# A kernel for graph diffusion, routed experts and segment paths: path columns packed two to a word and kept in registers

## The chip, the cores and the metric

One core of a Trainium2 chip runs the whole program. The metric is the device time of one execution in microseconds; of several executions the median counts.
## What is computed

The reference has four steps with a residual each. Cut to what matters here:

```python
x = x + gnn_diffusion(layernorm(x), ...)          # step 1
x = x + routed_experts(layernorm(x), ...)         # step 2
# step 3: 64 paths over 16 segments of 32 columns, for 4352 edges
x1 = x_nodes[src].reshape(-1, 16, 32)             # x_nodes = layernorm(x), 256 x 512
x2 = x_edges.reshape(-1, 16, 32)
i1, i2, i3 = path_indices[:, 0], path_indices[:, 1], path_indices[:, 2]
contrib = path_coeffs[None, :, None] * x1[:, i1, :] * x2[:, i2, :]
edge_out = zeros.at[:, i3, :].add(contrib)
out = zeros.at[dst].add(edge_out.reshape(-1, 512))
x = x + out
x = x + grouped_experts(layernorm(x), ...)        # step 4
```

The path indices are data: the kernel learns only at run time which segments a path reads and writes.

## The kernel before

The 4352 edges lie as 34 tiles of 128 edges, and step 3 works them in three blocks of 10, 14 and 10 tiles (`BLOCKS`, L35). For each block all 64 paths (`NP`) are worked in turn, so there are 192 path steps.

- VectorE multiplies (L744): the gathered node columns of segment i1, the edge columns of segment i2 and the path's coefficient go into one of seven slots of `prod` (`SLOTS`). Then it adds the slot's later tiles into the sums in on-chip memory (L758). It works multiply(p + 1) before add(p). A multiply waits until TensorE has used the slot seven paths back (`psums`); an add waits for the add before it (`sums`).
- TensorE adds the slot's first four tiles (L1042), in blocks 0 and 1 a fifth too (L1045), into banks of PSUM by an identity matmul at column i3, once the multiply is done (`mults`). Between paths it gathers node rows for the next block (L972, six matmuls a tile) and scatters the last block's sums to nodes (L993, four matmul records a tile), at path numbers fixed by `gather_paths` and `scatter_paths`: gathers after paths 3, 7, 11, 15, 20 and so on up to 58 in block 0; in block 1 a scatter after paths 1, 7, 13 and so on and a gather after paths 3, 9, 15 and so on, ten of each; in block 2 a scatter after paths 1, 5, 9 and so on.
- ScalarE copies gathered rows out of PSUM (L443), makes the one-hot matrices of the scatter (L448, L451), and between blocks copies the PSUM sums (L479, L483). TensorE closes a block with matmuls of zeros (L1055), waits for these copies and opens the next with matmuls of zeros (L1037).

The columns of a path come from registers. VectorE packs the three segment numbers of a path into one integer of three 9-bit fields, times 32 (L565 to L569). Each of the two engines loads 16 such words at a time into registers (`load_words`, L183): the first 16 ahead of the blocks, then VectorE at p % 16 == 4 (L765) and TensorE at p % 16 == 7 (L1053), twelve loads on each in all. `column` (L187) takes a field out with // and %, which become register operations of the sequencer, as does the address arithmetic around them. [...]

Ahead of step 2 TensorE works its last matmuls of step 1 (L928), then 34 small matmuls that only keep it busy (`keep_warm`, L850, called by `transpose_xn`, L855), and waits for the normalised rows that VectorE makes (L533) to transpose them (L858).

## Time and profile before

| | us |
|---|---|
| median of 3 executions (328.79 to 329.98) | 329.12 |
| the profiled execution's own time | 329.91 |
| its span, first to last instruction | 328.1 |
| PE matmul busy | 304.3 (93%) |
| DVE busy | 237.4 (72%) |
| ACT busy | 87.5 (27%) |
| path steps, block 0 | about 106 to 156 |
| path steps, block 1 | about 156 to 220.5 |
| path steps, block 2 | about 220.5 to 272 |

Busy shares are averages over stages with different limits, so they are read by stretch. Matmul ends are modelled: a matmul's duration overlaps the next one, and what one costs is read from start to start. The same holds for VectorE, whose instructions overlap at their ends.

### The profile page before, as it was taken

The numbers are of one execution on the slowest core, as the hardware profiler recorded it, in microseconds if no ns is written. First come the engines' busy times: TensorE is split into PE (matmuls) and PEld (weight loads), VectorE is DVE, ScalarE is ACT, GpSimd is POOL, SyncE is SP. The second block draws the span as 40 slices with busy tenths as digits, with TensorE's granted clock in tenths as the row PEclk, the third lists the DMA queues.
The fourth block names the chain that finished last, engine by engine and source line by source line (L and its number), as shares of the span: only waits on it lengthen the run. The fifth ranks groups of instructions, "written<-read, shape, count | busy, mean of one in ns | idle before, by whom it ended". The sixth has DMA issues, their size and how long they took to land.

```text
span 328.1 us, 5513 instructions
## 1 busy us (share of the span) xinstructions
PE 304.3 (93%) x1813; PEld 205.6 (63%) x1828; DVE 237.4 (72%) x637; ACT 87.5 (27%) x173; POOL 17.8 (5%) x24
## 2 busy tenths in 40 slices
PE   3898999999998998999799999988988998999996
PEld 2665598876443686877476766664655554477832
DVE  1998944121354999989999999997999995766131
ACT  3600241002115111211422222128322237512120
POOL 3000050000003000000000000030000004000000
PEclk9999999999999999999999999996999999999999
DMA  5999900000052000000000000019700007200001
GB/s 128 406 396 444 391 12 0 2 1 1 0 222 99 0 3 0 2 1 2 1 2 0 1 2 0 3 29 392 301 0 0 3 0 248 75 0 2 2 0 64
DMA packets 8845, 26.55 MB, mean 81 GB/s; under 512 B 2673, under 2 KB 2674, under 8 KB 7922
## 3 DMA queue, kind: packets, MB, share of 16 engines
q1 hardware_dynamic: 7328, 26.12, 20.6%
q8 instruction: 15, 0.25, 0.3%
q10 hardware_dynamic: 1490, 0.09, 0.3%
q14 instruction: 12, 0.10, 0.1%
HBM read 25.68 MB, written 0.52 MB: 80 GB/s over the span
## 4 chain that ended last, share of the span: by engine, by line
PE 78%; DVE 8%; ACT 4%; issue 3%; DVEq 2%; another core or an unknown queue 2%; DMA 1%; SPq 0%; ACTq 0%
PE psum L1042 14%; PE psum L993 12%; PE psum L972 12%; PE psum L946 9%; PE psum L1045 5%; PE psum L967 4%; PE psum L850 4%; DVE prod L744 3%; PE psum L882 2%; PE psum L1101 2%; PE psum L1126 2%; PE psum L1120 2%; PE psum L898 2%; ACT big L479 2%; DVE big L758 2%
## 5 line engine op out<-in xcount | busy, mean ns | idle before, releaser
L744 DVE SCALAR_TENSOR_TENSOR prod<-big,coef_b,edges 128x320 f32 (+1 forms) x192 | 113.2, 591 | 2.4 <-PE psum L1042 1.0
L1042 PE MATMUL psum<-prod,ident 128*128 128x128 f32 x384 | 77.0, 301 | 6.4 <-DVE prod L744 5.6
L758 DVE TENSOR_TENSOR big<-big,prod 128x160 f32 (+2 forms) x192 | 71.9, 374 | 7.7 <-issue 6.9
L1042 PEld LDWEIGHTS psum<-prod,ident 128*128 128x128 f32 x384 | 59.8, 192 | 26.6 <-issue 22.6
L993 PE MATMUL psum<-big,dst_oh 128*128 128x512 f32 x116 | 55.8, 607 | 0.4 <-ACT dst_oh L451 0.4
L972 PE MATMUL psum<-xparts,src_t 128*128 128x512 bf16 x192 | 45.9, 379 | 0.6
L1045 PE MATMUL psum<-prod,ident 128*128 128x32 f32 x256 | 39.3, 236 | 0.0
L1045 PEld LDWEIGHTS psum<-prod,ident 128*128 128x128 f32 x256 | 38.9, 192 | 0.0
L972 PEld LDWEIGHTS psum<-xparts,src_t 128*128 128x128 bf16 x204 | 20.3, 108 | 18.7 <-issue 0.6
L443 ACT ACTIVATE big<-psum 128x512 f32<-128x512 f32 x29 | 17.0, 598 | 56.2 <-PE psum L972 56.2
L993 PEld LDWEIGHTS psum<-big,dst_oh 128*128 128x128 f32 x116 | 20.4, 194 | 17.3 <-issue 14.7
L448 ACT ACTIVATE dst_oh<-iota_b,idx_f 128x256 f32<-128x256 bf16 x29 | 14.7, 505 | 60.2 <-PE psum L993 60.2
L946 PE MATMUL psum<-edges,big 128*128 128x256 f32 x128 | 28.6, 381 | 0.0
L946 PEld LDWEIGHTS psum<-edges,big 128*128 128x128 f32 x128 | 24.0, 190 | 3.8 <-DVE edges L696 0.3
L850 PE MATMUL psum<-iota_b,zero_b 128*128 128x256 bf16 x137 | 18.0, 284 | 0.0
L356 POOL MEMSET big<- 128x2560 f32 (+2 forms) x3 | 8.8, 2939 | 164.2 <-PE psum L993 112.7
L850 PEld LDWEIGHTS psum<-iota_b,zero_b 128*128 128x128 bf16 x137 | 13.8, 102 | 3.0 <-issue 0.7
L967 PE MATMUL psum<-big,edges 128*128 128x512 f32 x32 | 14.0, 596 | 0.0
L451 ACT ACTIVATE dst_oh<-dst_oh 128x256 f32<-128x256 f32 x29 | 12.1, 417 | 0.9
L967 PEld LDWEIGHTS psum<-big,edges 128*128 128x128 f32 x32 | 6.0, 190 | 7.5 <-issue 7.5
L696 DVE TENSOR_TENSOR edges<-edges,psum 128x256 f32<-128x256 f32 x8 | 3.2, 415 | 10.3 <-ACT edges L427 10.3
L427 ACT ACTIVATE edges<-psum 128x256 f32<-128x256 f32 x8 | 3.1, 383 | 26.3 <-PE psum L946 22.2
(167 smaller groups left out, 264.3 us busy)
## 6 DMA issues: line engine op xcount, KB each, us to landing
big<-in_w SPq DMA_DIRECT2D x3, 2048.0 KB, 19.2
edges<-in_edge SPq DMA_DIRECT2D x2, 2560.0 KB, 18.0
edges<-in_f SPq DMA_DIRECT2D x1, 4096.0 KB, 12.9
edges<-in_edge SPq DMA_DIRECT2D x1, 3584.0 KB, 23.2
edges<-in_f SPq DMA_DIRECT2D x1, 2560.0 KB, 9.9
edges<-in_f SPq DMA_DIRECT2D x1, 1536.0 KB, 17.2
big<-in_gnn_w SPq DMA_DIRECT2D x1, 1024.0 KB, 10.3
xs<-in_x SPq DMA_DIRECT2D x1, 512.0 KB, 5.2
```

Of the source, the lines that this page charges most:

```text
L443: nc.scalar.activation(x1g[b % 2][:, t - FIRST[b], :], gather_bank(t), ACT.Copy).then_inc(gathered, 1)
L448: nc.scalar.activation(to, iota_b[:], ACT.Abs, bias=idx_f[:, 0, t:t + 1]).then_inc(dist_made, 1)
L451: nc.scalar.activation(to, to, ACT.Relu, scale=-1.0, bias=1.0).then_inc(done, 1)
L744: nc.vector.scalar_tensor_tensor(out=prod[:, (p0 + p) % SLOTS, 0:tiles], in0=xg[:, 0:tiles, bass.ds(i1, U)], scalar=coef_b[:, p:p + 1], in ...
L758: nc.vector.tensor_tensor(v, v, prod[:, (p0 + p) % SLOTS, KEPT[b]:tiles], ALU.add).then_inc(sums, 1)
L850: mm(to[:, 0:N], zero_b[:], iota_b[:], start=True, stop=True)
L946: last = mm(bank[2 + c % 4][:, n * N:(n + 1) * N], w[:, kc, c * P:(c + 1) * P], xnT[:, kc, :], start=kc == 0, stop=kc == KC - 1)
L967: last = mm(bank[2 + h], hT[:, c, h * P:(h + 1) * P], w2_sb[:, c, :], start=c == 0, stop=c == HC - 1)
L972: last = mm(gather_bank(t), src_t[:, h, t * P:(t + 1) * P], xparts[:, k, h, :], start=h == 0 and k == 0, stop=h == H - 1 and k == 2)
L993: last = mm(bank[2 + h], dst_oh[:, n % DR, h * P:(h + 1) * P], tile_sums(b, t), start=n == 0, stop=False)
L1042: last = mm(path_sums(to), ident[:], prod[:, slot, 0:PT].rearrange("p t u -> p (t u)"), start=False, stop=False, skip_group_check=True)
L1045: last = mm(psum[:, bass.ds(to + 512, U)], ident[:], prod[:, slot, PT, :], start=False, stop=False, skip_group_check=True)
```

## The change

Two paths share a word: the packing uses fields of 4 bits (`SEG`), 12 bits a path, two paths side by side and all times 32, and needs one packing instruction more. There are 32 words (`path_pair`). Each engine loads all of them once, VectorE ahead of the first copies of gathered rows, TensorE ahead of `transpose_xn(1)`, where 24 small matmuls take the place of 34; all later loads are gone. `column` extracts with shifts and masks, in another form in each block (shift, then mask; mask, then shift; shift, mask, shift back), so that no extracted value is one that the program already has.

```diff
@@ -36,8 +36,10 @@
     FIRST = [0, 10, 24]
     KEPT = [5, 5, 4]
     PT = 4
-    SB = (NS * U).bit_length() - 1
-    PG = 16
+    SEG = (NS - 1).bit_length()
+    FIELD = (NS - 1) * U
+    PAIRS = NP // 2
+    assert U == 32
     NB = len(BLOCKS)
     QT = -(-T // 4)
     BMAX = max(BLOCKS)
@@ -77,6 +79,7 @@
         zero_b = sb("zero_b", [P, P], BF16)
         coef_b = sb("coef_b", [P, NP])
         path_w = sb("path_w", [1, NP], I32)
+        path_pair = sb("path_pair", [1, PAIRS], I32)
         idx_f = sb("idx_f", [P, 2, T])
         stats = sb("stats", [P, H, 6])
         mv = sb("mv", [P, H, 2])
@@ -177,21 +180,22 @@
         hid_bd = take([FC, NG * EQ])
         made_rows = take([QF, H, D])
 
-        def load_words(engine, words, n):
-
-            regs = [engine.alloc_register(f"{engine.engine.name}_word{i}") for i in range(n, n + PG)]
-            engine.load(regs, path_w[0:1, n % NP:n % NP + PG])
-            for i, r in enumerate(regs):
-                words[n + i] = engine.snap(r, donate=True, min_val=0, max_val=2 ** (3 * SB) - 1)
-
-        def column(words, n, k):
-
-            v = words[n]
-            if k:
-                v = v // 2 ** (SB * k)
-            if k < 2:
-                v = v % 2 ** SB
-            return nc.s_assert_within(v, 0, (NS - 1) * U,
+        def load_words(engine):
+            regs = [engine.alloc_register(f"{engine.engine.name}_word{i}") for i in range(PAIRS)]
+            engine.load(regs, path_pair[0:1, :])
+            return [engine.snap(r, donate=True, min_val=0, max_val=U * 2 ** (6 * SEG) - 1) for r in regs]
+
+        def column(words, b, p, k):
+
+            shift = SEG * (3 * (p % 2) + k)
+            v = words[p // 2]
+            if b == 0:
+                v = (v >> shift) & FIELD if shift else v & FIELD
+            elif b == 1:
+                v = (v & (FIELD << shift)) >> shift if shift else v & (FIELD + (1 << 29))
+            else:
+                v = ((v >> (shift + 5)) & (NS - 1)) << 5
+            return nc.s_assert_within(v, 0, FIELD,
                                       skip_runtime_bounds_check_because="segment numbers are below the segments")
 
         def scatter_order(b):
@@ -562,11 +566,15 @@
             nc.vector.tensor_scalar(idx_f[:, 0, :], idx_f[:, 1, :], -1.0, None, ALU.mult).then_inc(neg_ready, 1)
             dve.wait_ge(path_in, 16)
             pw = path_w[:].rearrange("o (n k) -> o n k", k=1)
-            link(nc.vector.scalar_tensor_tensor(out=pw, in0=path_i[:, :, 2:3], scalar=float(NS * U), in1=path_i[:, :, 1:2],
+            link(nc.vector.scalar_tensor_tensor(out=pw, in0=path_i[:, :, 2:3], scalar=float(NS), in1=path_i[:, :, 1:2],
                                                 op0=ALU.mult, op1=ALU.add))
-            link(nc.vector.scalar_tensor_tensor(out=pw, in0=pw, scalar=float(NS * U), in1=path_i[:, :, 0:1],
+            link(nc.vector.scalar_tensor_tensor(out=pw, in0=pw, scalar=float(NS), in1=path_i[:, :, 0:1],
                                                 op0=ALU.mult, op1=ALU.add))
-            nc.vector.tensor_scalar(pw, pw, float(U), None, ALU.mult).then_inc(packed, 1)
+            pp = path_pair[:].rearrange("o (n k) -> o n k", k=1)
+            two = path_w[:].rearrange("o (n k) -> o n k", k=2)
+            link(nc.vector.scalar_tensor_tensor(out=pp, in0=two[:, :, 1:2], scalar=float(NS ** 3), in1=two[:, :, 0:1],
+                                                op0=ALU.mult, op1=ALU.add))
+            nc.vector.tensor_scalar(pp, pp, float(U), None, ALU.mult).then_inc(packed, 1)
 
             for h in range(H):
                 dve.wait_ge(cnt_ps, 1)
@@ -722,8 +730,8 @@
                         .then_inc(part_r, 1)
 
 
-            words = {}
-            load_words(dve, words, 0)
+            dve.wait_ge(packed, 1)
+            words = load_words(dve)
             for t in range(1, BLOCKS[0], 2):
                 dve.wait_ge(gat_ps, t + 1)
                 nc.vector.tensor_copy(x1g[0][:, t, :], gather_bank(t)).then_inc(gathered_odd, 1)
@@ -737,7 +745,7 @@
 
                 def multiply(p):
 
-                    i1, i2 = column(words, p0 + p, 0), column(words, p0 + p, 1)
+                    i1, i2 = column(words, b, p, 0), column(words, b, p, 1)
 
                     if p0 + p >= SLOTS:
                         dve.wait_ge(psums, p0 + p + 1 - SLOTS)
@@ -748,7 +756,7 @@
 
                 def add(p):
 
-                    to = column(words, p0 + p, 2)
+                    to = column(words, b, p, 2)
 
                     if p == 0:
                         dve.wait_ge(mults, p0 + p + 1)
@@ -761,8 +769,6 @@
                 for p in range(NP):
                     if p + 1 < NP:
                         multiply(p + 1)
-                    if p % PG == 4 and (b, p) < (NB - 1, NP - PG):
-                        load_words(dve, words, p0 + (p // PG + 1) * PG)
                     add(p)
 
             for i in range(SPLIT + 1):
@@ -852,7 +858,7 @@
             def transpose_xn(stage):
                 for h in range(H):
                     if stage:
-                        keep_warm(bank[5], ((34, 6), (18, 12))[stage - 1][h])
+                        keep_warm(bank[5], ((24, 6), (18, 12))[stage - 1][h])
                     pe.wait_ge(xn_ready, H * (stage if stage < 2 else 3) + h + 1)
                     for kc in range(KC):
                         last = nc.tensor.transpose(bank[kc // 2][:, (kc % 2) * N + h * P:(kc % 2) * N + (h + 1) * P],
@@ -929,6 +935,8 @@
                 last.then_inc(diff_ps, 1)
 
 
+            pe.wait_ge(packed, 1)
+            words = load_words(pe)
             transpose_xn(1)
             pe.wait_ge(small_in, 16 * 5)
             for h in range(H):
@@ -1019,9 +1027,6 @@
                     gather_part(t, 1, k)
             for t in range(8, BLOCKS[0]):
                 gather(t)
-            pe.wait_ge(packed, 1)
-            words = {}
-            load_words(pe, words, 0)
             for b in range(NB):
                 gathers = list(range(FIRST[b + 1], FIRST[b + 1] + BLOCKS[b + 1])) if b + 1 < NB else []
                 scatters = scatter_order(b - 1) if b else []
@@ -1036,7 +1041,7 @@
                 for q in sum_banks(b):
                     mm(bank[q], zero_b[:], src_t[:, 0, 0:512], start=True, stop=False)
                 for p in range(NP):
-                    to = column(words, NP * b + p, 2)
+                    to = column(words, b, p, 2)
                     pe.wait_ge(mults, NP * b + p + 1)
                     slot = (NP * b + p) % SLOTS
                     last = mm(path_sums(to), ident[:], prod[:, slot, 0:PT].rearrange("p t u -> p (t u)"),
@@ -1049,8 +1054,6 @@
                         scatter(b - 1, *scatters[scatter_at.index(p)])
                     if p in gather_at:
                         gather(gathers[gather_at.index(p)])
-                    if p % PG == 7 and (b, p) < (NB - 1, NP - PG):
-                        load_words(pe, words, NP * b + (p // PG + 1) * PG)
                 for q in sum_banks(b):
                     mm(bank[q], zero_b[:], src_t[:, 0, 0:512], start=False, stop=True).then_inc(block_ps, 1)
             pe.wait_ge(sums, NP * NB)
```

## Rows read from the trace of the kernel before

**Rows 1.** Busy time by stretch: start:end, length, engine busy (x instructions), granted clock, DMA.

```profile
220.00:227.00 7.00, 6.06 (x19) 2.94 (x18) 6.11 (x16) 6.19 (x14) 0.00 (x0) 0.51 0.92 331
```

**Rows 2.** The same, block 1; busy are PE, PEld, DVE, ACT and POOL.

```profile
156.00:220.50 64.50, 60.92 (x362) 43.55 (x366) 62.40 (x128) 17.77 (x35) 2.66 (x1) 1.00 0.00 1
```

**Rows 3.** The word loads of L183 on VectorE's sequencer: duration ns min/median/max, first and last start.

```profile
L183 DVEq TENSOR_LOAD <-path_w x12: 1097/1100/1360, 97.0 to 250.6; - x12
```

**Rows 4.** VectorE's timeline, block 0 around a load: start, duration, idle before in brackets.

```profile
108.76 0.55 DVE L744 SCALAR_TENSOR_TENSOR prod<-big,coef_b,edges 128x320 f32 x1
...
109.46 0.55 DVE L744 SCALAR_TENSOR_TENSOR prod<-big,coef_b,edges 128x320 f32 x1
110.74 0.33 DVE L758 TENSOR_TENSOR big<-big,prod 128x160 f32 x1 [0.74 <-issue]
111.10 0.55 DVE L744 SCALAR_TENSOR_TENSOR prod<-big,coef_b,edges 128x320 f32 x1
```

**Rows 5.** The chain of waits, block 0, gathers: start, duration, what.

```profile
126.89 1.29 PE psum L972 x6
...
129.89 1.29 PE psum L972 x6
...
133.38 1.24 PE psum L972 x5
```

**Rows 6.** TensorE's timeline, block 0, its first gather.

```profile
109.27 0.59 PE L972 MATMUL psum<-xparts,src_t 128*128 128x512 bf16 x2
```

**Rows 7.** The chain of waits, from block 0's last gather into block 1.

```profile
152.36 1.29 PE psum L972 x6
...
155.81 0.23 PE psum L1055
...
160.74 1.80 PE psum L993 x4
...
166.35 1.80 PE psum L993 x4
```

**Rows 8.** VectorE's timeline, end of block 1 and start of block 2.

```profile
217.81 0.68 DVE L744 SCALAR_TENSOR_TENSOR prod<-big,coef_b,edges 128x448 f32 x1
...
218.77 0.68 DVE L744 SCALAR_TENSOR_TENSOR prod<-big,coef_b,edges 128x448 f32 x1
...
220.59 0.55 DVE L744 SCALAR_TENSOR_TENSOR prod<-big,coef_b,edges 128x320 f32 x1
```

**Rows 9.** VectorE's timeline, the last two multiplies of block 2.

```profile
270.19 0.55 DVE L744 SCALAR_TENSOR_TENSOR prod<-big,coef_b,edges 128x320 f32 x1
...
270.92 0.55 DVE L744 SCALAR_TENSOR_TENSOR prod<-big,coef_b,edges 128x320 f32 x1
```

**Rows 10.** The chain of waits, end of block 1 and start of block 2.

```profile
220.27 0.39 PE psum L1055
...
223.29 1.89 PE psum L1037 x4
...
228.31 0.89 PE psum L1042 x8
```

**Rows 11.** VectorE's timeline, block 2, its tenth multiply.

```profile
228.92 0.55 DVE L744 SCALAR_TENSOR_TENSOR prod<-big,coef_b,edges 128x320 f32 x1 [0.99 <-PE psum L1042]
```

**Rows 12.** Register instructions by line: duration ns min/median/max, first and last start.

```profile
L758 DVEq FUSED_REGOPS  x192: 110/115/115, 106.8 to 271.8; - x192
L1045 PEldq FUSED_REGOPS  x128: 51/51/57, 107.0 to 219.7; - x128
```

**Rows 13.** The chain of waits, the 34 small matmuls ahead of step 2.

```profile
37.80 3.71 PE psum L850 x34
```

**Rows 14.** VectorE's timeline, its first copies of gathered rows.

```profile
101.19 2.49 DVE L729 COPY big<-psum 128x512 f32<-128x512 f32 x4 [3.55 <-PE psum L972]
```

**Rows 15.** VectorE's timeline, the normalised rows that TensorE's transposes wait for.

```profile
40.49 0.55 DVE L533 TENSOR_SCALAR xn<-xs,mv,rstd 128x512 f32<-128x512 f32 x1
```

**Rows 16.** VectorE's timeline, the first work behind the packing.

```profile
24.30 0.76 DVE L573 TENSOR_SCALAR edges<-psum 128x256 bf16<-128x256 f32 x2 [0.25 <-PE psum L882]
```

## The prediction

> **What bounds the kernel now.** The busy times by stretch come first. TensorE's granted clock is 0.51 from 220 to 227 us, its halved level [rows 1]; in all other stretches of the path stage it is 1.00. The change touches that stage (192 paths, three blocks of 64): in block 1 (156 to 220.5 us) TensorE is busy for 60.9 and VectorE for 62.4 of 64.5 us [rows 2]. Two engines are near full side by side, so a gain on one is worth only what the other lets through. The word loads stand in the view of their line: twelve on each engine, of 1.10 us each with 16 words [rows 3]. VectorE's timeline tells what one costs. A multiply follows the last after 0.70 us (108.76 to 109.46), but after 1.64 us (109.46 to 111.10) where a load lies between [rows 4], with 0.74 us idle "issue" before the add: 0.94 us more. The engine can't run ahead of a load, because the add behind it waits for the add before it. The first load lies ahead of the loops; eleven are inside. On TensorE a load lies behind a gather or scatter that was issued just before, and it stalls nothing there.
>
> Whether that VectorE time is on the path is read from the chain of waits. In block 0 TensorE's gathers begin 3.00 us apart (126.89, 129.89) with four paths between and 3.49 us (129.89, 133.38) with five [rows 5]. That is 0.73 us a path against VectorE's 0.70. TensorE is the slower one and only waits where a load has stopped VectorE. In block 1 one scatter, one gather and six paths take 5.62 us (160.74 to 166.35) [rows 7], 0.94 us a path, against 0.96 us on VectorE (217.81 to 218.77) [rows 8]: a tie. In block 2 VectorE paces with 0.73 us (270.19 to 270.92) [rows 9].
>
> **Block 0 after the change.** The four loads in it go, 4 x 0.94 = 3.8 us on VectorE. The next late thing is TensorE. Its first gather begins at 109.27 [rows 6]. Of the 13 distances between 14 gathers ten hold four paths and three hold five: 10 x 3.00 + 3 x 3.49 = 40.5, so the last gather begins at 149.8 instead of 152.36. From there to the last path's end it takes 3.45 us (152.36 to 155.81) [rows 7]. End: 153.2, that is 2.6 us earlier, not 3.8. VectorE is ahead of that: 64 multiplies at 0.70 from 106 on end near 150.8, or 151.3 with two short hiccups as now.
>
> **Block 1.** From the end of block 0's paths to the first scatter it is 4.93 us (155.81 to 160.74): closing matmuls, ScalarE's five copies, opening matmuls, two paths [rows 7]. So the scatter begins at 158.1. Ten cycles of 5.61 and two last paths of 0.45 end at 158.1 + 56.1 + 0.9 = 215.1, where the chain now has 220.27 [rows 10]. VectorE's last multiply of block 0 begins near 150.4 and the first of block 1 some 1.8 us later, as at the next change of blocks (218.77 to 220.59) [rows 8]: 152.2. Its last one begins 0.6 + 62 x 0.965 later, at 212.6; with its 0.68 us and some 0.8 for TensorE's path behind it that is 214.1. TensorE is late by 1.0 us more, so 215.1 stands: 5.2 us earlier than now. Here the tie turns, and TensorE stays dense up to the block's end.
>
> **Block 2.** Now it is 8.04 us from 220.27 to the first scatter's end at 228.31, with the four opening matmuls taking 1.89 us at the halved clock [rows 10]; then a path of 0.22 and 0.39 us until VectorE's tenth multiply at 228.92, which the view shows waiting for TensorE (0.99 us idle, L1042) [rows 11]. So the first load of this block is hidden already. With a full clock the same stretch is block 1's 4.93 less one opening matmul (0.22) and with two paths of 0.22 for those of 0.81 in all: 4.35; scatter 1.72, path 0.22, release 0.39: 6.7 instead of 8.65. Then 54 multiplies of 0.732 and some 0.6 of hiccups as now: 40.1, against 42.0 with two loads in them (228.92 to 270.92) [rows 9, 11]. The last multiply begins at 215.1 + 6.7 + 40.1 = 261.9, 9.0 us earlier. If the clock halves as now, it is 215.1 + 8.65 + 40.1 = 263.85, 7.1 us earlier. I take the full clock: the fall came after a stretch in which TensorE worked paths alone at VectorE's 0.96 us, and the like boundary between blocks 0 and 1, behind dense work, has full clock and a stop of some 3 us too.
>
> **The extraction.** Each of the three forms adds register operations: two for every column in blocks 0 and 1 (one where the shift is zero), three in block 2, where a column had a modulo, a division or both. [...]
>
> [...]
>
> **Loads in their new places.** 32 words: between 1.1 us (no cost by word) and 2.7 us (twice the slowest, 1.36 [rows 3]); 2.2 taken. VectorE's goes before the first gather copies, where the engine idles for 3.55 us [rows 14]: nothing. TensorE's goes behind the matmuls of L928, which run up to 37.80; their last wait ends well before, so they are queued and the load should run beside them. Behind it wait the warm-up matmuls and the transposes. Those warm-ups fall from 34 (3.71 us, to 41.5) to 24: 2.6 us, to 40.4 [rows 13]. VectorE's xn starts at 40.49 and takes 0.55 us [rows 15], so with 0.2 us of release the transposes start near 41.3 and not at 41.5: 0.2 us gained. Were the load exposed, up to 1.6 us would be lost (2.7 + 2.6 - 3.7). The third packing step adds about 0.27 us, and VectorE idles for 0.25 us before L573 [rows 16]: 0.1 us lost at most. Sum of the front: -0.1.
>
> [...]
>
> **The sum.** Block 0 -2.6, block 1 -2.6, block 2 -1.9 (start, clock) and -1.9 (loads), front -0.1: -9.1 us. All behind the last multiply keeps its length: transfers of ctrl, f1 and f2 are issued by multiply counts and move along. The profiled execution took 329.91 us (span 328.1), so 320.8; it lies 0.8 above the median of 329.12, which gives 320.0. I forecast 320.2, nearer to the median's.
>
> **Rivals.**
> - The clock still halves, at block 2 or at another pause that shifts against it. For it: the pauses of 2.9 us stay, and clock rows of one execution don't show how near the others were. It costs 1.9 us at block 2, up to 3 in the tail: 322 to 323.5. Chance 0.22.
> - TensorE's load is exposed in the front: 321.5 to 322. Against it: loads inside the blocks ran beside queued matmuls. 0.06.
> - Slower than before: shifts and masks cost as a division. [...] It decides once the sequencer's share of a path exceeds what VectorE's own 0.73 us cover; no gain is left at 9.1 / 54 = 0.17 us a path. If the new operations aren't fused but issued one by one, it is worse still, past 345. Together 0.09.
> - The change does less than it says: registers run short and are copied, or a block's tie holds on VectorE through hiccups, and only the loads on the path go: 324 to 328. 0.08.
> - Loads are hidden already, so nothing is gained: 329. [...] The timeline speaks against it. 0.02.
>
> **How the numbers follow.** The forecast's own case (318.5 to 321.5) has 0.53. The range of 317.7 to 325.5 adds the clock, the exposed load and half of the fourth. A measurement tells 0.5% (1.6 us) from no change. Faster by more than that: 0.53 + 0.22 + 0.06 + 0.06 = 0.87; within it 0.04; slower 0.09.
>
> **What would show it.** No load inside the blocks; multiplies 0.70, 0.96 and 0.73 us apart with no pause of 0.9; TensorE without waits for VectorE in block 0 after the first gather; block 0's paths ending near 153, block 1's near 215, the last multiply near 261.9; no halved clock at block 2. Wrong would be: multiplies in block 2 over 0.75 us apart, fused instructions longer than 115 ns before an add, or a pause before L850 near 37.6 us.

## The result, and the profile after

The changed kernel takes 335.57 us (median, 335.44 to 335.68), against 329.25 for the kernel before (328.79 to 329.98): a ratio of 1.019, 95% interval 1.018 to 1.0205. It is slower, by 1.9%; the forecast was 320.2, 2.7% faster. The profiled execution took 335.44 us with a span of 333.7, so 5.5 us more than the profiled execution of before (329.91).

The rows of after that answer those of before:

| | before, us | forecast | after |
|---|---|---|---|
| block 0's closing matmul starts | 155.81 | 153.2 | 158.32 |
| block 1's closing matmul starts | 220.27 | 215.1 | 221.32 |
| last multiply of block 2 starts | 270.92 | 261.9 | 276.14 |
| clock at 220 to 227 us | 0.51 | 1.00 | 1.00 |

Busy time by stretch (start:end, length, busy of PE, PEld, DVE, ACT, POOL, granted clock, DMA), for [rows 1]:

```profile
220.00:227.00 7.00, 4.88 (x25) 2.81 (x25) 6.29 (x15) 5.33 (x12) 0.00 (x0) 1.00 0.76 272
```

The word loads by line (duration ns min/median/max, first and last start), for [rows 3]. They are long as taken (2.2 us), and there is one on each engine:

```profile
L185 PEldq TENSOR_LOAD <-path_pair x1: 2317/2317/2317, 34.8 to 34.8; - x1
L185 DVEq TENSOR_LOAD <-path_pair x1: 2353/2353/2353, 97.1 to 97.1; - x1
```

The chain of waits (start, duration, what) at the two changes of blocks, for [rows 7, 10]:

```profile
158.32 0.23 PE psum L1058
...
163.25 1.80 PE psum L1001 x4
...
221.32 0.23 PE psum L1058
...
224.18 1.04 PE psum L1042 x4
```

From the closing matmul to the first scatter it is still 4.93 us (158.32 to 163.25), and block 2's four opening matmuls take 1.04 us instead of 1.89, at full clock. The structure between the blocks is what the forecast said (`psum L1047` and `L1050` are TensorE's adding of a path, L1058 the closing and L1042 the opening matmuls, L1001 the scatter). What is wrong lies inside them. VectorE's timeline, multiplies of block 0 for [rows 4] and the last one of block 2 for [rows 9]:

```profile
119.72 0.55 DVE L752 SCALAR_TENSOR_TENSOR prod<-big,coef_b,edges 128x320 f32 x1
...
120.43 0.55 DVE L752 SCALAR_TENSOR_TENSOR prod<-big,coef_b,edges 128x320 f32 x1
...
121.29 0.55 DVE L752 SCALAR_TENSOR_TENSOR prod<-big,coef_b,edges 128x320 f32 x1
...
122.00 0.55 DVE L752 SCALAR_TENSOR_TENSOR prod<-big,coef_b,edges 128x320 f32 x1
...
276.14 0.55 DVE L752 SCALAR_TENSOR_TENSOR prod<-big,coef_b,edges 128x320 f32 x1
```

There is no load there any more, and still the multiplies of block 0 follow each other after 0.71 and 0.86 us in turn (119.72, 120.43, 121.29, 122.00) where it was 0.70, and after 0.84 us in block 2 (273.61 to 274.45 below) where it was 0.73. The register instructions of block 0 by line, for [rows 12] (duration ns min/median/max), the multiply's of before (L744; its add is the line of [rows 12]), then those of after (L752 is the multiply's line, L766 the add's):

```profile
L744 DVEq FUSED_REGOPS  x70: 72/210/246, 105.8 to 156.9; - x70
...
L744 DVEq ALU_OP  x64: 40/40/52, 106.1 to 154.1; - x64
```

```profile
L752 DVEq ALU_OP  x160: 40/40/57, 106.0 to 156.6; - x160
L752 DVEq FUSED_REGOPS  x128: 53/70/116, 106.1 to 156.7; - x128
...
L766 DVEq ALU_OP  x126: 45/45/45, 107.0 to 156.9; - x126
L766 DVEq FUSED_REGOPS  x63: 65/65/72, 107.1 to 157.0; - x63
```

No view names the operations in a register instruction; the counts of the runs tell. With the masks ahead (below) L746 writes each mask as a register operation by itself, two a path, and the line has 142 ALU_OPs for 70 multiplies and no other register instruction; with three more such masks a path (below) L757 has 180 for 60. So an ALU_OP is one register operation here. With division and modulo (below) the three columns of a path in block 0 are written with nine operations and come with three FUSED_REGOPS and no ALU_OP (128 and 63 for 64 paths). So a FUSED_REGOPS, fused for short, holds several.

In block 0 of the changed kernel there are 4.5 ALU_OPs a path (160/64 and 126/63) beside three fused instructions. The kernel before had three register instructions in all there: one fused of 210 ns and one ALU_OP of 40 ns for the multiply, one fused of 115 ns for the add. (So an ALU_OP needs no mask; in blocks 1 and 2 the kernel before has none: 118 and 116 fused ones and no other on L744 from 158 to 218 and from 224 to 272 us.) Of the changed kernel's operations a path of an even number has three masks and two shifts and makes four ALU_OPs; a path of an odd number has three of each and makes five. That fits each mask (AND), the add's shift, and the multiply's shift where it comes ahead of the first mask; between the two masks of the multiply, where the second column's shift is written, stands one fused instruction. With mask first (below), three masks a path and every shift behind its mask, there are 183 ALU_OPs for 61 multiplies and 60 adds (106 to 152 us), three a path. So in these kernels no AND was seen to join a fused instruction, and it splits the group that it stands in: a multiply has two fused instructions here (128 for 64), and one where its masks are written elsewhere (73 on L756 for 70, below).

What this does is in the chain of waits of block 2, from one multiply's start to the next (start, duration, what):

```profile
273.61 0.08 DVE prod L752
273.69 0.03 issue
273.72 0.04 DVEq L766
273.77 0.03 issue
273.80 0.07 DVEq L766
273.87 0.09 issue
273.96 0.04 DVEq L752
274.01 0.03 issue
274.04 0.04 DVEq L752
274.08 0.14 DVE big L766
274.22 0.04 issue
274.26 0.04 DVEq L752
274.30 0.03 issue
274.33 0.07 DVEq L752
274.40 0.05 issue
274.45 0.08 DVE prod L752
```

In 0.84 us the chain stays with the sequencer's instructions (DVEq) and the 0.03 to 0.09 us ahead of each; the engine's own multiply and add appear as stubs of 0.08 and 0.14. In block 2 VectorE doesn't pace its paths any more, the instruction stream does. (In block 0 it does so at every second path, the one of 0.86 us.) Of the whole chain DVEq has 5% after (2% before) and "issue" 7% (3%).

### The profile page after: what moved, and what is told of

Its sections match the earlier page's. It is cut to its first block, busy times and chain, and to the rows that moved or that the text cites. A ratio compares the mean times of both kernels' runs of the same rounds, so it can differ in the third digit from the quotient of the medians.

```text
span 333.7 us, 6607 instructions
## 1 busy us (share of the span) xinstructions
PE 305.7 (92%) x1818; PEld 204.5 (61%) x1818; DVE 244.3 (73%) x638; ACT 87.5 (26%) x173; POOL 17.8 (5%) x24
## 4 chain that ended last, share of the span: by engine, by line
PE 68%; DVE 14%; issue 7%; DVEq 5%; ACT 3%; DMA 2%; SPq 0%; ACTq 0%
PE psum L980 13%; PE psum L1047 12%; PE psum L954 8%; PE psum L1001 8%; PE psum L1050 5%; PE psum L975 4%; DVEq L752 3%; DVE big L766 3%; PE psum L1104 2%; PE psum L856 2%; PE psum L1129 2%; PE psum L1123 2%; DVE big L547 2%; DVE big L549 2%; DVE prod L752 2%
## 5 line engine op out<-in xcount | busy, mean ns | idle before, releaser
L752 DVE SCALAR_TENSOR_TENSOR prod<-big,coef_b,edges 128x320 f32 (+1 forms) x192 | 114.0, 594 | 7.6 <-issue 2.0
L1047 PE MATMUL psum<-prod,ident 128*128 128x128 f32 x384 | 79.4, 303 | 9.8 <-DVE prod L752 7.5
L1047 PEld LDWEIGHTS psum<-prod,ident 128*128 128x128 f32 x384 | 60.2, 190 | 32.0 <-issue 27.0
L766 DVE TENSOR_TENSOR big<-big,prod 128x160 f32 (+2 forms) x192 | 71.9, 374 | 1.2 <-DVE big L766 0.9
L1001 PE MATMUL psum<-big,dst_oh 128*128 128x512 f32 x116 | 55.2, 601 | 0.5 <-ACT dst_oh L455 0.5
L980 PE MATMUL psum<-xparts,src_t 128*128 128x512 bf16 x204 | 48.1, 379 | 0.0
L1050 PE MATMUL psum<-prod,ident 128*128 128x32 f32 x256 | 39.3, 236 | 0.0
L1050 PEld LDWEIGHTS psum<-prod,ident 128*128 128x128 f32 x256 | 38.9, 192 | 0.0
L1001 PEld LDWEIGHTS psum<-big,dst_oh 128*128 128x128 f32 x116 | 20.0, 191 | 17.1 <-issue 14.3
L856 PE MATMUL psum<-iota_b,zero_b 128*128 128x256 bf16 x127 | 16.8, 283 | 0.0
L856 PEld LDWEIGHTS psum<-iota_b,zero_b 128*128 128x128 bf16 x127 | 12.7, 102 | 2.8 <-issue 0.7
```

The source lines that it names most:

```text
L752: nc.vector.scalar_tensor_tensor(out=prod[:, (p0 + p) % SLOTS, 0:tiles], in0=xg[:, 0:tiles, bass.ds(i1, U)], scalar=coef_b[:, p:p + 1], in ...
L766: nc.vector.tensor_tensor(v, v, prod[:, (p0 + p) % SLOTS, KEPT[b]:tiles], ALU.add).then_inc(sums, 1)
L856: mm(to[:, 0:N], zero_b[:], iota_b[:], start=True, stop=True)
L980: last = mm(gather_bank(t), src_t[:, h, t * P:(t + 1) * P], xparts[:, k, h, :], start=h == 0 and k == 0, stop=h == H - 1 and k == 2)
L1001: last = mm(bank[2 + h], dst_oh[:, n % DR, h * P:(h + 1) * P], tile_sums(b, t), start=n == 0, stop=False)
L1047: last = mm(path_sums(to), ident[:], prod[:, slot, 0:PT].rearrange("p t u -> p (t u)"), start=False, stop=False, skip_group_check=True)
```

## The experiments

The pace tells most of each run: mean and median distance between the starts of two multiplies of a block, 63 distances each. All kernels hold 0.965 us (median) in block 1, where the instructions are longer (a multiply 0.68 us for 0.55, before). Where short and long distances take turns the median hides them, so the text then gives both.

| kernel | block 0 mean (median) | block 2 mean (median) | us | ratio to before, 95% |
|---|---|---|---|---|
| before | 0.762 (0.698) | 0.799 (0.731) | 329.25 | |
| after | 0.800 (0.782) | 0.863 (0.844) | 335.57 | 1.018 to 1.0205 |
| constant columns | 0.694 (0.698) | 0.744 (0.731) | 319.52 | 0.969 to 0.972 |
| forms, loads kept | 0.829 (0.783) | 0.919 (0.841) | 343.72 | 1.042 to 1.0454 |
| mask first | 0.750 (0.735) | 0.771 (0.754) | 326.42 | 0.989 to 0.992 |
| division, modulo | 0.756 (0.748) | 0.804 (0.786) | 328.02 | 0.994 to 0.997 |
| mask first, dear form in block 1 | 0.750 (0.737) | 0.770 (0.753) | 327.16 | one time |
| constant on TensorE | 0.799 (0.782) | 0.863 (0.843) | 334.57 | 1.016 to 1.021 |
| constant on VectorE | 0.694 (0.698) | 0.744 (0.731) | 320.01 | 0.970 to 0.974 |
| two layouts | 0.734 (0.723) | 0.779 (0.760) | 326.42 | 0.990 to 0.993 |
| masks ahead | 0.704 (0.698) | 0.745 (0.731) | 321.63 | 0.976 to 0.979 |
| three more behind multiply | 0.853 (0.829) | 0.900 (0.876) | 340.63 | 1.032 to 1.037 |
| three more behind add | 0.856 (0.833) | 0.903 (0.912) | 342.25 | 1.0365 to 1.040 |
| loads of 1 word | 0.915 (0.907) | 0.937 (0.927) | 346.29 | 1.050 to 1.0535 |
| loads of 2 words | 0.855 (0.931) | 0.884 (0.951) | 340.34 | 1.032 to 1.035 |
| loads of 4 words | 0.755 (0.703) | 0.787 (0.734) | 327.91 | one time |

**The two halves of the change apart.** The change takes the loads out of the loops and changes how a column is extracted. First the loads' removal alone: no extraction at all, every column a constant, so the sums are not those that the data ask for, and the address arithmetic goes too (no register instruction is left in the loops).

```diff
-            shift = SEG * (3 * (p % 2) + k)
-            v = words[p // 2]
-            ...
+            return U * ((5 * p + 3 * k) % NS)
```

> The kernel after, with every column a constant of the program (so other columns than the data ask for are used): no extraction and no address arithmetic on any sequencer, the words still loaded once. Theory 1 (VectorE's sequencer paces blocks 0 and 2, because masks go out as instructions of their own beside the fused ones): multiplies 0.70, 0.96 and 0.73 us apart, block 0's paths end near 153, the last multiply near 262, total 320 to 321. Theory 2 (the time is lost elsewhere: in the front with its 2.3 us load, in TensorE's path, in the block changes): over 328, pace of blocks 0 and 2 still near 0.79 and 0.85 us.

Measured: 319.52 us (319.38 to 320.12), ratio 0.970. The chain of waits has the closing matmul of block 1:

```profile
214.88 0.23 PE psum L1049
```

and VectorE's timeline the last multiply:

```profile
260.72 0.53 DVE L743 SCALAR_TENSOR_TENSOR prod<-big,coef_b,edges 128x320 f32<-128x320 f32 x1
```

That is 214.9 against 215.1 forecast, and 260.7 against 261.9. The forecast except for the extraction is borne out, and the price of the register work in the changed kernel is 335.6 - 319.5 = 16.1 us: (0.800 - 0.694) x 63 = 6.7 us in block 0, (0.863 - 0.744) x 63 = 7.5 in block 2, 1.0 at the two changes of blocks, the rest ahead of the first multiply (0.3) and behind the last. That the kernel with constant columns has no address arithmetic either isn't what makes it fast: the fastest kernel below extracts everything and gets to 321.6.

Then the other half alone: the kernel before with its loads of 16 words, one path a word, but 4-bit fields and the three forms.

```diff
-            v = words[n]
-            if k:
-                v = v // 2 ** (SB * k)
-            if k < 2:
-                v = v % 2 ** SB
+            shift, b = SEG * k, n // NP
+            v = words[n]
+            if b == 0:
+                v = (v >> shift) & FIELD if shift else v & FIELD
+            elif b == 1:
+                v = (v & (FIELD << shift)) >> shift if shift else v & (FIELD + (1 << 29))
+            else:
+                v = ((v >> (shift + 5)) & (NS - 1)) << 5
```

> The kernel before with its sixteen-word loads inside the blocks, but fields of 4 bits and the three forms of the kernel after: the extraction alone. Theory 1: block 2 goes to 0.84 us a path, block 0 stays near 0.71 (its words have no second path, the dear one), so 335 to 338. Theory 2: 329, as before.

Measured: 343.72 us (343.37 to 344.09), ratio 1.044. VectorE's timeline, block 0:

```profile
120.64 0.55 DVE L748 SCALAR_TENSOR_TENSOR prod<-big,coef_b,edges 128x320 f32 x1
...
121.34 0.55 DVE L748 SCALAR_TENSOR_TENSOR prod<-big,coef_b,edges 128x320 f32 x1
...
122.13 0.55 DVE L748 SCALAR_TENSOR_TENSOR prod<-big,coef_b,edges 128x320 f32 x1
```

In block 2 the median pace is that of the changed kernel (0.841 and 0.844), so there the pairs in a word cost nothing and the forms everything. In block 0 the equal medians (0.783 and 0.782) mislead. The distances here are 0.70 and 0.79 in turn (120.64, 121.34, 122.13), a mean of 0.745, and in the changed kernel 0.71 and 0.86, a mean of 0.785. A path of its own word has seven register instructions, since its column 0 needs no shift; the second path of a pair has eight. So in block 0 the pairs cost 0.04 us a path, about half of what the changed kernel loses there beyond 0.70. It missed the expected 335 to 338: the forms cost 14.5 us here over division and modulo, nearly as much as all register work costs without loads (16.1), and taking the loads out saves 8.2 us with these forms, where going from before to constant columns saves 9.7. I had expected the two costs to hide in each other; they nearly add, as both are time of one sequencer. (Its profiled execution also has a granted clock of 0.50 from 129.3 to 132.7 us, where VectorE paces.)

**Which engine.** Constant columns on one engine only, the changed kernel's extraction on the other. First TensorE's loop:

```diff
-                    to = column(words, b, p, 2)
+                    to = U * ((5 * p + 6) % NS)
```

> The changed kernel with every column constant on TensorE only; VectorE extracts its three columns a path as in the changed kernel (so the sums are not those of the data). Theory: the 16 us between the changed kernel (335.6) and the one with constant columns on both engines (319.5) are VectorE's, whose multiply and add alternate without slack in blocks 0 and 2; TensorE's one column a path is extracted while it waits for the multiply. Then 333.5 to 336, and a pace of about 0.80 and 0.86 us in blocks 0 and 2. Rival: both engines pay a share because they release each other (the multiply waits for the path sums of 24 paths back): then in between, 325 to 331.

Measured: 334.57 us (334.42 to 336.37), ratio 1.018. Then VectorE's multiply and add:

```diff
-                    i1, i2 = column(words, b, p, 0), column(words, b, p, 1)
+                    i1, i2 = U * ((5 * p) % NS), U * ((5 * p + 3) % NS)
-                    to = column(words, b, p, 2)
+                    to = U * ((5 * p + 6) % NS)
```

> The changed kernel with every column constant on VectorE only; TensorE extracts as in the changed kernel (the sums are not those of the data). Theory that the cost is VectorE's: 319.5 to 321. Rival, a share of TensorE's: 324 to 330. The two runs of this pair should add up: the two savings together are near 16 us if the costs are separate, and less than 16 if one hides the other.

Measured: 320.01 us (319.64 to 320.3), ratio 0.972. (A multiply waits for the sums of seven paths back; the 24 in the first of these two expectations is a slip.) VectorE's extraction is worth 15.6 us, TensorE's 1.0 or 0.5, and the two savings add up to 16.6 against 16.1. It is VectorE's, but for 1 us at most.

**Cheaper forms.** Mask first in every block, so that the AND stands alone and what is behind it fuses. Spare bits in the mask, always zero in a word, make the value another one in each block, as the three forms did.

```diff
+            spare = (0, 1 << 29, 1 << 30)[b]
+            v = words[p // 2] & ((FIELD << shift) + spare)
+            if shift:
+                v = v >> shift
```

> The kernel after, with the form of block 1 (mask, then shift) in all three blocks, kept distinct by a spare bit in the mask (bit 29 or 30, which no word has). Two mask instructions fewer or shifts out of the singles: by theory 1 and the trace of after, a path needs 0.07 us less of VectorE's sequencer in block 0 and 0.14 us less in block 2, so multiplies are 0.70 to 0.72 and 0.73 to 0.75 us apart and the total is 320 to 323. Theory 2: 333 to 336, as after.

Measured: 326.42 us (325.9 to 326.82), ratio 0.990. This is 9.2 us under the changed kernel, but above the 320 to 323 expected: six register instructions a path are still too many. Division and modulo alone in blocks 0 and 2, which come in fused instructions only, as the rows below show (`low` is shift + 5, the bits below the field; the topmost column of block 0 has a form of its own, left out here):

```diff
-                v = (v >> shift) & FIELD if shift else v & FIELD
+                v = v % 2 ** (low + SEG) // 2 ** low * U
...
-                v = ((v >> (shift + 5)) & (NS - 1)) << 5
+                v = v // 2 ** low % NS * U
```

> The kernel after, with modulo, division and a product by 32 in blocks 0 and 2 (all of them inside fused instructions; block 1 keeps mask and shift). Theory 1: no single instructions in blocks 0 and 2, 0.42 to 0.52 us of sequencer a path, so the engine paces with 0.70 and 0.73 us: 320 to 322. If divisions are dear enough to pace, 0.75 us in block 2 and 322 to 325. Theory 2: 333 to 336.

Measured: 328.02 us (327.93 to 329.13), ratio 0.996; the expected 320 to 322, or 322 to 325, are missed too. All register instructions of block 0 (L754 the multiply, L768 the add):

```profile
L754 DVEq FUSED_REGOPS  x128: 115/162/260, 106.6 to 154.6; - x128
```

```profile
L768 DVEq FUSED_REGOPS  x63: 159/171/192, 107.7 to 154.8; - x63
```

There is no ALU_OP, and three instructions a path as in the kernel before, but they take 162 ns twice and 171 ns where those took 210, 40 and 115. The pace is between mask-first's and the changed kernel's. So what counts is the time of the instructions, not only how many there are. In the last of this group mask first stands in blocks 0 and 2 (the part left out) and the dearest form in block 1:

```diff
+            if b == 1:
+                v = ((v >> (shift + 5)) & (NS - 1)) << 5
+            else:
+                ...
```

> The kernel after with the forms moved: block 1 gets the dearest (shift, mask, shift back), blocks 0 and 2 mask and shift. If a form costs only what exceeds the cover of VectorE's own work in that block (0.70, 0.96 and 0.73 us a path), block 1 keeps 0.965 us a path under the form that gave 0.845 in block 2, and the total is that of e2_mask_first, 325.5 to 327.5. If a form adds its time wherever it stands, block 1 goes to 1.05 us or more and the total to 331 or more.

Measured: 327.16 us, one time, 0.7 above mask first. Block 1's median stays 0.965 us and its mean goes from 0.969 to 0.987, by five pauses of 0.34 us (of which more at the end). The form that costs 0.09 us a path more than mask first in block 2 (0.844 against 0.754) costs 0.02 where VectorE's own two instructions take 0.97.

**Count or place.** The masks of the multiply after next are written into registers of their own, right behind the multiply's issue and ahead of the add's arithmetic. The add's first register instruction waits for the add before it (`sums`), and there the sequencer stood idle until 0.04 us behind that add's end (mask first, more below); also, without an AND between them, both columns of a multiply are finished by one fused instruction (73 on L756 for 70 multiplies).

```diff
+                def masks(p):
+                    out = []
+                    for k in range(2):
+                        r = dve.alloc_register(f"masked{b}_{p}_{k}")
+                        dve.reg_alu(r, words[p // 2], (FIELD << SEG * (3 * (p % 2) + k)) + (0, 1 << 29, 1 << 30)[b], ALU.bitwise_and)
+                        out.append(dve.snap(r, donate=True, min_val=0, max_val=U * 2 ** (6 * SEG) - 1))
+                    return out
...
                     if p + 1 < NP:
-                        multiply(p + 1)
+                        multiply(p + 1, masked)
+                    if p + 2 < NP:
+                        masked = masks(p + 2)
                     add(p)
```

> Mask first, with one difference: the two masks of the multiply after next are written into registers ahead of the add, so that they stand in the long shadow of the multiply (0.55 us) and not in the short one of the add (0.32 us); both columns of a multiply are then finished by one fused instruction. The work of the sequencer shrinks a little (one instruction a path fewer), its place changes. Theory (what counts is what stands between an add and the next multiply, beyond what the add covers): pace 0.70 to 0.72 in block 0 and 0.73 to 0.75 in block 2, 320.5 to 323. Rival (the sum of the sequencer's instructions a path decides, wherever they stand): 325 to 326.5.

Measured: 321.63 us (321.53 to 321.85), ratio 0.977 (0.976 to 0.979). It beats both kernels, with the full computation. VectorE's timeline and register instructions of block 0 (L746 the masks ahead, L756 the multiply, L770 the add):

```profile
120.37 0.55 DVE L756 SCALAR_TENSOR_TENSOR prod<-big,coef_b,edges 128x320 f32 x1
...
121.07 0.55 DVE L756 SCALAR_TENSOR_TENSOR prod<-big,coef_b,edges 128x320 f32 x1
```

```profile
L746 DVEq ALU_OP  x142: 40/40/57, 106.0 to 156.8; - x142
...
L756 DVEq FUSED_REGOPS  x73: 59/142/171, 106.2 to 156.6; - x73
...
L770 DVEq ALU_OP  x68: 40/40/40, 107.0 to 156.1; - x68
L770 DVEq FUSED_REGOPS  x68: 90/95/107, 107.1 to 156.2; - x68
```

The pace is VectorE's own again, 0.70 us, as with constant columns. This run changes two things: the place of two instructions, and their number (five a path in block 0 for mask-first's six). To part them, three more masks a path were added to it, in two places (`again`: two more ANDs of column 0, one of column 1). They keep the bits that are there, so no value changes; the two kernels have equally many instructions.

```diff
+                def again(p, masked):
+                    ...
-                        masked = masks(p + 2)
+                        masked = again(p + 2, masks(p + 2))
```

> The kernel with the masks ahead, and three more masks a path on VectorE (the same bits again, so values don't change), behind the multiply's issue and ahead of the add's arithmetic. Each takes 0.04 us and 0.03 to the next, 0.21 us a path together. Theory (place decides): in the kernel with the masks ahead the sequencer waits there for the multiply to start, some 0.12 us of it, and behind that its chain from a multiply's start to the next one's has 0.14 us of slack against 0.70. So nearly all of the three is covered: pace 0.70 to 0.71 and 0.73 to 0.74 us, 321.6 to 324 with somewhat more of the periodic pauses. Rival (the count decides): as in the partner run, 327 to 330.

Measured: 340.63 us (340.2 to 341.44), ratio 1.034.

```diff
                     add(p)
+                    if p + 2 < NP:
+                        masked = again(p + 2, masked)
```

> The same three masks a path, behind the add's issue and ahead of the multiply's arithmetic, all else as in the partner run. Theory (place decides): there they lie on the chain from one multiply's start to the next, 0.56 us now, so 0.77: pace 0.76 to 0.79 us in blocks 0 and 2, (0.07 + 0.05) x 63 = 7.6 us more, 328 to 330. Rival (neither the place nor three masks matter, the gain came from the spared instruction): 321.6 to 324 in both runs.

Measured: 342.25 us (341.43 to 342.42), ratio 1.038. The added masks of block 0 (L757 in both), first behind the multiply, then behind the add:

```profile
L757 DVEq ALU_OP  x180: 40/40/40, 106.4 to 156.6; - x180
```

```profile
L757 DVEq ALU_OP  x177: 40/40/40, 106.8 to 156.6; - x177
```

My theory of the place fell, and both kernels lie 10 us or more above every range that I had given. The pace of block 0 is 0.829 and 0.833 us, the same in both places; in block 2 the means are 0.900 and 0.903 (there the second's distances are 0.84 and 0.92 in turn, so its median misleads). From masks ahead to three more behind the multiply the means rise by 0.149 and 0.155 us, which are 19.1 us over the two blocks, all of the 19.0 between the two kernels. The 1.6 us between the two places are 0.4 ahead of the first multiply, 0.2 in block 0, 0.2 in block 2 and 0.8 in block 1, where the masks behind the add leave five pauses of some 0.25 us and those behind the multiply none. So in block 1 the place does matter, by 0.8 us. (The second's granted clock is 0.50 from 225.0 to 228.4 us, but its last multiply of block 1 is 1.47 us late already, 224.05 against 222.58.) The chain of waits with the masks behind the multiply (block 2) tells what one costs:

```profile
276.83 0.04 DVEq L757
276.87 0.03 issue
276.90 0.04 DVEq L757
276.94 0.03 issue
276.97 0.04 DVEq L757
```

One starts 0.07 us after the other (276.83, 276.90, 276.97). Three are 0.21 us, so without them a path's sequencer work sums to an estimated 0.829 - 0.21 = 0.62 us in block 0. That is 0.08 under VectorE's 0.70, and this slack is all there was. So the sum over all register instructions of a path decides here: the pace is the larger of VectorE's own 0.70 (0.73 in block 2) and that sum. A wait of the sequencer may add to it; mask first points that way below. The step that failed in the first of these expectations is the 0.14 us of slack. I had added up only the chain behind a multiply's start (0.56) and taken the masks ahead of it as free.

Place can matter where the sequencer would wait. In mask first the step is 0.764 us at every second path and 0.706 at the others, and the add's mask starts 0.04 us behind the end of the add before, for which it waits (`sums`): some 0.12 us behind the multiply's start at the long ones, 0.05 at the short ones. That points to the wait, but no run takes it away alone. How much of the 4.8 us from mask first to masks ahead is the wait and how much the spared instruction stays open.

**Two layouts.** VectorE keeps 47 words (`MIX` is 15): 30 paths have nine-bit fields of their own, opened by division and modulo in blocks 0 and 2, and 34 lie in pairs, mask first.

```diff
+            if two and p % 4 < 2 and p // 4 < MIX:
+                v = words[2 * (p // 4) + p % 4]
+                ...
+            else:
+                ...
```

> VectorE keeps 47 registers instead of 32: 30 of the 64 paths have a word of their own in nine-bit fields, which division and modulo open in one fused instruction, 34 share a word in pairs and are opened mask first; no load stands in the loop, TensorE has pairs as before. Theory (a path of its own word runs at the kernel before's 0.70 us in block 0 and 0.73 in block 2, a path of a pair at mask-first's 0.75 and 0.77): 319.5 plus about half of mask-first's 6.9, so 322 to 324. Rival, that the pace follows the slowest form because the two alternate: 325.5 to 327. The 15 more words of the load cost about 1 us on an engine that waits for the gathers there: nothing at the end.

Measured: 326.42 us (326.32 to 326.6), ratio 0.992: no better than mask first alone. It missed 322 to 324. The pace (0.723 median in block 0) does lie between the two forms. VectorE's load begins 1.3 us later than in the changed kernel (98.4 against 97.1), and the first multiply is 1.3 us later too (107.7 against 106.4); I had put that at nothing. It isn't the longer load: VectorE still idles for 3.55 us ahead of its first copies. The five more packing steps of 0.16 to 0.19 us are in the chain of waits near 25 us, and xn is 1.3 us late already (42.17 against 40.86). The fused instructions of the nine-bit paths take up to 267 ns. In block 2 the mean (0.779) is no lower than mask-first's.

**What a load costs by its size.** The kernel before with VectorE's 16-word loads in pieces of `FEW` = 1, 2 and 4 words, each two paths ahead of its use.

```diff
-                    if p % PG == 4 and (b, p) < (NB - 1, NP - PG):
-                        load_words(dve, words, p0 + (p // PG + 1) * PG)
+                    if (p + 2) % FEW == 0 and p0 + p + 2 not in words and p0 + p + 2 < NP * NB:
+                        load_words(dve, words, p0 + p + 2, FEW)
```

> The kernel before, in which VectorE loads one word on each path instead of sixteen on each sixteenth; extraction and TensorE's loads as before. A load of 16 words takes 1.10 us and one of 32 takes 2.32, so the time goes by the word (0.076 us) with next to nothing for the load itself; a path's own register work leaves VectorE's sequencer some 0.15 us of cover in blocks 0 and 2 (0.94 us of stall for a load of 1.10). So 0.08 us of load and 0.07 to issue it are just hidden: no stalls, 0.70 to 0.71 and 0.73 to 0.75 us a path, 319 to 323. If a load has a fixed part of some 0.2 us or more, the pace goes to 0.85 us and the total to 335 or more.

> The same with two words on each second path: 0.15 us of load and 0.07 to issue against 0.15 of cover, 0.07 us a pair of paths exposed at most: 320 to 324. With a fixed part of 0.2 us: 326 to 330, less than with single words.

> The same with four words on each fourth path: 0.30 us of load, some 0.2 us exposed each time in blocks 0 and 2: pace 0.75 us on the mean in block 0 and 0.78 in block 2, 323 to 327.

Measured: 346.29 us (345.96 to 347.36) with one word, 340.34 (339.99 to 340.91) with two, 327.91 with four. VectorE's loads by line, in this order:

```profile
L184 DVEq TENSOR_LOAD <-path_w x191: 296/303/781, 97.9 to 287.1; - x191
```

```profile
L184 DVEq TENSOR_LOAD <-path_w x96: 523/527/778, 97.9 to 279.7; - x96
```

```profile
L184 DVEq TENSOR_LOAD <-path_w x48: 340/342/596, 97.4 to 264.5; - x48
```

One word takes 0.30 us, two 0.53, four 0.34, sixteen 1.10 [rows 3], thirty-two 2.32 to 2.35. By the word alone a single one would have been 0.07 us. With one word the second case of its expectation came true (a fixed part, 335 or more); two words, at 340, missed both of theirs (320 to 324, 326 to 330); four words have the pace expected and lie 0.9 us above the range. Neither a price by the word nor one with a fixed part fits all five sizes. Four words at a time cost 0.25 us or less of stall (the mean pace of block 0 is 0.755 against 0.703 median, one load in four paths: 0.2 us) and are worth 1.3 us against loads of sixteen (one time). Why four words are faster than two isn't settled; no run varied the address at which a load begins.

## Why the prediction was wrong

- **The removal of the loads, all three blocks** (-2.6, -2.6, -1.9): right. With constant columns blocks 0 and 1 end at 152.97 and 214.9 us (forecast 153.2 and 215.1), and the whole takes 319.5 against 320.0. TensorE was named as the one that paces block 0 then, and with constant columns it does: the chain of waits has its gathers 3.00 us apart with four paths between (112.19, 115.19, 118.19), as forecast, and nothing of VectorE from 106 us to the block's end. The kernel with the masks ahead, which computes everything, has its last multiply at 262.25 us against 261.9 forecast.
- **The clock** (-1.9): right. It stays at its full level over the change from block 1 to block 2, in the changed kernel (1.00 from 220 to 227 us) and in the one with the masks ahead (1.00 from 215 to 263 us); the changed kernel's opening matmuls take 1.04 us.
- **The front** (-0.1): nearly. The first multiply starts at 106.41 us against 106.20, so 0.2 lost; with the same front it is 106.10 with constant columns and 106.66 in another kernel, so 0.2 is within what one execution tells. TensorE's load of 2.32 us begins at 34.8 and delays nothing: the last matmuls of step 1 run beside it from 34.51 to 38.18, and the 24 small ones start at 38.02 and end at 40.8. But VectorE's xn begins at 40.86 instead of 40.49, where 0.1 had been allowed for the packing, so the transposes start at 41.46 as before and the 0.2 us hoped for there are gone. VectorE's load lies in the idle time before its first copies, still 3.55 us [rows 14].
- **The extraction** (nothing): this is the step that failed. I took a shift or a mask to be fused and no dearer than the operations that it stands in for, so that the sequencer's share of a path falls in every block. That was my estimate, and no row shows it: [rows 12] time fused instructions of the kernel before, which takes its columns with // and % and has no AND, and not the single operations in them. Measured, the masks come as ALU_OPs, 0.04 us long and 0.07 from start to start (L757 above), and split the group around them. A path in block 0 has 7.5 register instructions instead of three. The share rose: in block 2 it is 0.84 us after (the pace itself, as the chain there holds little else), and before it fitted under VectorE's 0.73.
- **The cover.** That VectorE paces block 2 with its own 0.73 us held before the change, with little in hand. The sum of the kernel with the masks ahead is 0.62 us with five instructions (the estimate above, block 0), so only 0.08 are free even there. No row told how much of the sequencer's share is covered, and the forecast took the whole as covered.
- **The rival that held** was the second half of the one at 0.09: not fused but issued one by one. Its size, past 345, was too high, since part of the sum lies under VectorE's work; without loads 335.6. It counted on block 2 alone, where 0.17 us a path would take the whole gain. Measured are 0.119 there, which alone would not have been enough, and 0.106 in block 0, for which it gives no number: together 14.2 us against a gain of 9.1.

Against the kernel before the time goes so. Block 0's last multiply starts 2.6 us later, since the forms cost more than the four loads did. Block 1 gives 1.6 us back (its last one is 0.95 late), as its loads are gone and its long instructions cover the forms. Block 2 loses 4.3 us (276.14 against 270.92, 5.2 late).

## What to carry to other kernels

Where an engine's instructions have addresses from registers and its own work takes under a microsecond a step, add up the sequencer's register instructions of a step from start to start, and compare the sum with the engine's pace; here it was a bound of its own (0.84 us in block 2 against 0.73), and its instructions filled the chain of waits where it was the bound. Count in the trace which operations fuse: here a path with // and % had three fused instructions and no ALU_OP, and one with three & had three ALU_OPs more. Take one register instruction more as the 0.07 us a step measured here on VectorE until a row says otherwise, and keep expensive forms for stages whose long instructions cover them. Issuing it where the sequencer would wait may help; no run here shows that by itself.

## What the runs showed of the hardware that I had not expected

- A register operation issued alone on VectorE's sequencer (ALU_OP) takes 0.04 us and 0.07 from start to start (L757 above), while a fused instruction that finishes the add's whole address takes 0.095 (L770 above).
- A load of four words from on-chip memory into registers (0.34 us) is shorter than one of two (0.53).
- The instruction stream has pauses. In block 0 of the changed kernel a multiply comes some 0.35 us late at about every thirteenth path (timeline of VectorE, and the instruction queue's transfers over 106 to 157 us: packets, MB, share):

```profile
146.17 0.55 DVE L752 SCALAR_TENSOR_TENSOR prod<-big,coef_b,edges 128x320 f32 x1
...
147.39 0.55 DVE L752 SCALAR_TENSOR_TENSOR prod<-big,coef_b,edges 128x320 f32 x1 [0.43 <-PE psum L1050]
```

```profile
q14 instruction: 4, 0.03, 0.2%
```

The view names TensorE, but the register instructions of this multiply start at 146.9 us only, 0.44 us behind the add's last where other paths have 0.09; the sequencer itself comes late. There are four such pauses and four transfers in that stretch, and four and four in block 2; together some 2.9 us of the 16. With constant columns block 0 has none (665 VectorE records in the trace instead of 2041), with eight register instructions a path it has five of 0.35 us. With the masks ahead there are four transfers and only two pauses, of 0.23 us; slack may hide part of them. The count of the pauses goes roughly with that of the instructions. What causes them stays open. It isn't a wait for the transfer beside it: no transfer falls between 146.0 and 147.39 us, the next starts at 147.62, and of the changed kernel's eight one starts 0.1 us ahead of the late multiply and seven behind it, by 0.2 to 2.5 us.
